# A decoder layer on one core: input squares made as the input arrives, and short chains moved in five stages

## The reference, cut to what matters

```python
h_norm = _rmsnorm(h, norm1_w)                       # decay attention
q, k = _l2norm(h_norm @ u), _l2norm(h_norm @ v)     # 16 columns each
out = gate * _causal_conv(h_norm, k_base_kernel) + einsum(A, h_norm)   # A: q k, times gamma ** distance
h2 = h + out @ proj_w.T + proj_b
x = _layernorm(x + h2 + gelu(_rmsnorm(h2, norm2_w) @ mlp_w1 + mlp_b1) @ mlp_w2 + mlp_b2)
...
Pn = _rmsnorm(P, input_norm_w)                      # cross attention: keys and values of the context,
                                                    # then 3 rounds of scores, softmax over rows, GRU
x = _layernorm(x + slots)
...
probs = softmax(x @ router_w + router_b + expert_bias)   # 8 experts, the best 2 for each row, gates normed
x = _layernorm(x + sum of gate * (gelu(x @ W1 + B1) @ W2 + B2))
```

## Time and profile before

| | us |
|---|---|
| median of 3 runs (range) | 1296.32 (1294.4 to 1298.52) |
| the profiled execution | 1293.76 |
| its span, first to last instruction | 1292.1 |
| PE, DVE, ACT, POOL busy | 1173.5, 892.4, 616.5, 258.4 |
| attention and MLP | 0 to 202 |
| context | 202.6 to 231.5 |
| three rounds of cross attention | 232 to 941.8 |
| route | 942.1 to 972 |
| experts | 972.7 to 1268 |
| combine | 1269 to 1292.1 |

### The profile page before, as it was taken

One profiled execution on the slowest core, in us unless ns is written; L12 is line 12 of the kernel. 1 busy time (PEld: TensorE's weight loads), 2 busy tenths in 40 slices (PEclk: granted clock), 3 DMA queues, 4 the chain that ended last, 5 costly groups with the idle time before them and its releaser, 6 DMA issues. The chain is left out here.

```text
span 1292.1 us, 19037 instructions
## 1 busy us (share of the span) xinstructions
PE 1173.5 (91%) x6332; PEld 982.0 (76%) x6332; DVE 892.4 (69%) x1935; ACT 616.5 (48%) x1043; POOL 258.4 (20%) x302
## 2 busy tenths in 40 slices
PE   7988998799999999999999999999736999999990
PEld 5557884688778877878787787778636999999990
DVE  4646667698745669874556987457575888888883
ACT  4345636254434344443443444433305676676672
POOL 3016001000000000000000000000024767767751
PEclk8978998899999999999999999999857999999995
DMA  7010001000010000001000000081291222322324
GB/s 285 1 51 1 33 18 65 1 1 1 1 33 1 17 9 1 1 1 27 7 17 9 1 1 1 1 337 54 71 320 31 47 41 41 49 41 41 49 33 138
DMA packets 47983, 60.54 MB, mean 47 GB/s; under 512 B 15151, under 2 KB 39153, under 8 KB 47025
## 3 DMA queue, kind: packets, MB, share of 16 engines
q1 hardware_dynamic: 37856, 45.27, 10.3%
q0 software_dynamic: 8832, 12.11, 6.0%
q10 hardware_dynamic: 1232, 2.36, 0.5%
HBM read 45.25 MB, written 14.47 MB: 46 GB/s over the span
## 5 line engine op out<-in xcount | busy, mean ns | idle before, releaser
L76 PE MATMUL x_psum<-x_sn_lo,x_kq_hi 128*128 128x512 f32 (+1 forms) x312 | 126.4, 405 | 8.2 <-PEq L1372 6.8
L76 PE MATMUL x_psum<-x_p_lo,x_v_hi 128*128 128x512 f32 (+1 forms) x312 | 125.6, 402 | 5.1 <-DVE x_p_lo L1039 5.1
L77 PE MATMUL x_psum<-x_sn_hi,x_kq_lo 128*128 128x512 f32 (+1 forms) x312 | 124.6, 399 | 0.0
L78 PE MATMUL x_psum<-x_sn_hi,x_kq_hi 128*128 128x512 f32 (+1 forms) x312 | 124.0, 397 | 0.0
L77 PE MATMUL x_psum<-x_p_hi,x_v_lo 128*128 128x512 f32 (+1 forms) x312 | 123.5, 396 | 0.0
L78 PE MATMUL x_psum<-x_p_hi,x_v_hi 128*128 128x512 f32 (+1 forms) x312 | 122.7, 393 | 0.0
L947 ACT ACTIVATE x_e<-x_e,x_inv 128x1024 f32<-128x1024 f32 (+1 forms) x39 | 44.9, 1152 | 141.7 <-DVE x_inv L1060 141.7
L76 PE MATMUL e_bank<-e_w_lo,e_g_hi 128*128 128x256 f32 x368 | 107.9, 293 | 0.1
L76 PE MATMUL e_bank<-e_xT_lo,e_w_hi 128*128 128x256 f32 x368 | 105.1, 286 | 2.1 <-DVE e_xT_lo L1879 1.4
L77 PE MATMUL e_bank<-e_xT_hi,e_w_lo 128*128 128x256 f32 x368 | 104.8, 285 | 0.0
L78 PE MATMUL e_bank<-e_xT_hi,e_w_hi 128*128 128x256 f32 x368 | 104.8, 285 | 0.0
(11 more groups left out here) (395 smaller groups left out, 3169.6 us busy)
## 6 DMA issues: line engine op xcount, KB each, us to landing
w<-in_w SPq DMA_DIRECT2D x16, 1024.0 KB, 11.0
x_E_first<-scratch_row_inv SPq DMA_DIRECT2D x3, 1024.0 KB, 4.7
sT<-in_xT ACTq DMA_DIRECT2D x4, 512.0 KB, 12.1
a_x<-in_x SPq DMA_DIRECT2D x4, 512.0 KB, 7.8
scratch_x<-a_h SPq DMA_DIRECT2D x4, 512.0 KB, 2.6
w<-scratch_total SPq DMA_DIRECT2D x4, 512.0 KB, 5.7
out<-w SPq DMA_DIRECT2D x4, 512.0 KB, 2.8
y_cxT<-in_y_cxT SPq DMA_DIRECT2D x1, 1601.0 KB, 19.5
```

The lines of the kernel that those rows point to most:

```text
L76: pe.matmul(out, w_hi, x_lo, start=start, stop=False)
L77: pe.matmul(out, w_lo, x_hi, start=False, stop=False)
L78: return pe.matmul(out, w_hi, x_hi, start=False, stop=stop)
```

## The change

1. Input squares: ACT makes those of chunks 0, 2 and 3, between its exponentials and as the chunks arrive, DVE those of chunk 1, before it waits for POOL's constants. The roots of the rows get a chain of their own, before the raw queries are read, and ACT's scaled copies wait for `qk_sb` also.
2. MLP: `second_norm(c + 1)` stands after f = 2 of chunk c (c = 1, 2) on DVE and `normed(c + 1)` after f = 3 on ACT, in place of `second_norm(c + 2)`, `normed(c + 2)` in the second product of chunk c. `last_norm` stands after f = 4.
3. Context: `wh_hi` is made after `keys_hi(2)` and `wh_lo` is POOL's first work; the bias sums come after the last `norm.spread`; DVE's eight tiles of `v_lo` are split in six and two, around `keys_lo(6)` and `(7)`.
4. Route: ACT issues the write of the gates, and makes a Gelu of one column behind it; two of the nine last steps are left in the chain, two others follow unchained, and the rest goes to the start of the experts' stage on DVE, with a wait of POOL (`row_ok`) before its first `give`.
5. Combine: one chain for 16 tiles; ACT scales the first two tiles of each chunk, DVE the last two.
6. Some tiles and semaphores of the experts' stage are allocated earlier, in `program`.

```diff
+        ON_VECTOR = range(TPC, 2 * TPC)
+        ON_SCALAR = NT - TPC
...
+            def x_squares(c):
+                act.wait_ge(ld_x[c // 2], 32)
+                for t in range(c * TPC, (c + 1) * TPC):
+                    act.activation(h2[:, t], x[:, t], ACT.Square, accum_out=ss[:, t:t + 1]).then_inc(squares, 1)
+
+            x_squares(0)
             act.wait_ge(expos, 1)
             act.activation(lg[:], lg[:], ACT.Ln).then_inc(gammas, 1)
+            x_squares(2)
             act.wait_ge(expos, 2)
             act.activation(kw[:], kw[:], ACT.Exp).then_inc(gammas, 1)
...
-            for t in range(NT // 2):
-                act.wait_ge(ld_x[t // (NT // 2)], 32)
-                act.activation(h2[:, t], x[:, t], ACT.Square, accum_out=ss[:, t:t + 1]).then_inc(squares, 1)
-
+            x_squares(3)
             act.wait_ge(rs_ok, 1)
+            act.wait_ge(qk_sb, 1)
...
+                    if f == 3 and 1 <= c < NC - 1:
+                        normed(c + 1)
...
-                    normed(c + 2)
...
+            v.wait_ge(ld_x[0], 32)
+            for t in ON_VECTOR:
+                v.scalar_tensor_tensor(out=h2[:, t], in0=x[:, t], scalar=1.0, in1=x[:, t], op0=ALU.mult, op1=ALU.mult,
+                                       accum_out=ss[:, t:t + 1]).then_inc(vsquares, 1)
             v.wait_ge(consts, 1)
...
-            v.wait_ge(squares, NT // 2)
-            v.wait_ge(vsquares, NT // 2)
+            v.wait_ge(squares, ON_SCALAR)
+            v.wait_ge(vsquares, len(ON_VECTOR))
             k.step(v.tensor_scalar(sums[:, 0:NT], ss[:], 1.0 / D, EPS_RMS, ALU.mult, ALU.add))
+            rsqrt_steps(v, k, rs[:], sums[:, 0:NT], tmp[:, 0:NT])
+            v.sem_inc(rs_ok, 1)
             k.step(v.reciprocal(inv_ms[:], sums[:, 0:NT]))
...
-                rsqrt_steps(v, k, roots[:, done], sums[:, done], tmp[:, done])
+                rsqrt_steps(v, k, roots[:, ps], sums[:, ps], tmp[:, ps])
...
-                    if f == 3 and c >= 1:
+                    if f == 2 and 1 <= c < NC - 1:
+                        second_norm(c + 1)
+                    if f == 4 and c >= 1:
                         last_norm(c - 1)
...
-                    if t == c * TPC and c + 2 < NC:
-                        second_norm(c + 2)
...
         def _(pool):
+            pool.wait_ge(wh_hi_ok, 1)
+            pool.tensor_tensor(wh_lo[:], whT[:], wh_hi[:].bitcast(F32), ALU.subtract).then_inc(wh_lo_ok, 1)
             pool.wait_ge(v_hi_ok, 2)
...
             keys_hi(2)
+            act.wait_ge(ld_g, 48)
+            act.activation(wh_hi[:], whT[:], ACT.Copy).then_inc(wh_hi_ok, 1)
             keys_hi(3)
...
             norm.spread(v, slot_rs, 3, 3)
+            v.wait_ge(ld_g, 48)
+            k.mark(v.tensor_tensor(bias[:, 0:2 * DH], bi[:, 0:2 * DH], bi[:, 3 * DH:5 * DH], ALU.add))
+            k.mark(v.tensor_copy(bias[:, 2 * DH:3 * DH], bi[:, 2 * DH:3 * DH]))
+            k.mark(v.tensor_copy(bias[:, 3 * DH:], bi[:, 5 * DH:]))
             keys_lo(3)
...
+            v.wait_ge(v_hi_ok, 1)
+            rows_lo(0, 6)
             for i in range(6, len(keys)):
                 keys_lo(i)
...
+            rows_lo(6, 8)
...
-            sp.wait_ge(gate_ok, TOP)
-            sp.dma_start(io["x2"][:, D:].rearrange("(t p) k -> p t k", p=P), gates[:]).then_inc(gate_out, 16)
             sp.wait_ge(gate_out, 16)
...
             act.activation(pr[:], lg[:], ACT.Exp).then_inc(exp_ok, 1)
+            act.wait_ge(gate_ok, TOP)
+            act.dma_start(io["x2"][:, D:].rearrange("(t p) k -> p t k", p=P), gates[:]).then_inc(gate_out, 16)
+            act.activation(warm[:], ones[:, 0:1], ACT.Gelu)
...
+            k.step(v.tensor_scalar(found_i[:], bank[7][:, 0:PLACES], -1.0, None, ALU.add))
+            k.mark(v.tensor_scalar(token_of[:], found_i[:], T - 1, None, ALU.bitwise_and))
+            v.tensor_scalar(found[:], bank[7][:, 0:PLACES], -1.0, None, ALU.add)
+            v.scalar_tensor_tensor(out=empty[:], in0=bank[7][:, 0:PLACES], scalar=0.0, in1=spare[:], op0=ALU.is_equal, op1=ALU.mult)
...
+            pool.wait_ge(row_ok, 4)
             give(0, 0)
...
+            v.tensor_scalar(second[:], found[:], float(T), None, ALU.is_ge).then_inc(row_ok, 1)
+            v.tensor_scalar(first[:], found[:], float(T), None, ALU.is_lt).then_inc(row_ok, 1)
+            v.tensor_copy(row_f[:], token_of[:]).then_inc(row_ok, 1)
+            v.wait_ge(row_ok, 3)
+            v.wait_ge(ld_e, 16 * (2 * NE + 2))
+            v.tensor_tensor(row_of[:], row_f[:], empty[:], ALU.add).then_inc(row_ok, 1)
...
-            for h, tiles in enumerate(HALVES):
-                act.wait_ge(norm_ok, h + 1)
-                for t in tiles:
+            act.wait_ge(norm_ok, 1)
+            for c in range(NC):
+                for t in range(c * TPC, c * TPC + TPC // 2):
                     act.activation(x2[:, t], x2[:, t], ACT.Identity, bias=nb[:, t:t + 1], scale=rs[:, t:t + 1]).then_inc(out_ok, 1)
...
+            norm_of_stats(v, k, list(range(NT)), mark, stats, mv, rs, tmp, nb, norm_ok)
+            v.wait_ge(norm_ok, 1)
+            for c in range(NC):
+                for t in range(c * TPC + TPC // 2, (c + 1) * TPC):
+                    v.tensor_scalar(x2[:, t], x2[:, t], rs[:, t:t + 1], nb[:, t:t + 1], ALU.mult, ALU.add).then_inc(more_ok, 1)
```

More of the change, by code:

```diff
@@ L333, in cx_squares_of @@
                 act.wait_ge(ld_cx, 32)
-                act.wait_ge(squares, NT // 2 + (c + 3) * TPC)
+                act.wait_ge(squares, ON_SCALAR + (c + 3) * TPC)
                 for m in some:
@@ L418, in queries_and_keys @@
                 ps = slice(NT + g * NT, NT + (g + 1) * NT)
-                done = slice(0 if g == 0 else ps.start, ps.stop)
                 pairs = qk[:, ts].rearrange("p t a r -> p (t a) r")
@@ L474, in second_norm @@
                 sl = slice(c * TPC, (c + 1) * TPC)
-                v.wait_ge(squares, NT // 2 + (c + 1) * TPC)
+                v.wait_ge(squares, ON_SCALAR + (c + 1) * TPC)
                 k.step(v.tensor_scalar(ss[:, sl], ss[:, sl], 1.0 / D, EPS_RMS, ALU.mult, ALU.add))
@@ L1414, in _ @@
             rows_hi(1)
-            act.wait_ge(ld_g, 48)
-            act.activation(wh_hi[:], whT[:], ACT.Copy).then_inc(wh_hi_ok, 1)
             for i in range(6, len(keys)):
@@ L1525, in route @@
     gate = [gates[:, :, i] for i in range(TOP)]
-    second, first = shared["second"], shared["first"]
+    found, empty = shared["found"], shared["empty"]
     w2, b1, b2, ld_e = (shared[n] for n in ("w2", "b1", "b2", "ld_e"))
@@ L1739, in experts @@
         room = sT[:].rearrange("p c (a n) -> p (c a) n", n=CH)
-        xg = [room[:, 2 * i:2 * i + 2].rearrange("p a n -> p (a n)")[:, 0:SH * (D + TOP)].rearrange("p (s d) -> p s d", s=SH) for i in range(2)]
+        xg = shared["xg"]
         y = [room[:, 4 + i].rearrange("p (s d) -> p s d", s=SH) for i in range(2)]
         g32 = [room[:, 6 + i].rearrange("p (f n) -> p f n", f=2) for i in range(2)]
-        second, first = shared["second"], shared["first"]
+        second, first, found, empty = shared["second"], shared["first"], shared["found"], shared["empty"]
         share = sb("share", [P, 2, 2, SH])
         shared_ok, summed = sem("shared_ok"), sem("summed")
-        tokens, rows = sb("tokens", [P, 2 * SH], I32), sb("rows", [P, 2 * SH], I32)
-        tokens_ok, rows_ok = sem("tokens_ok"), sem("rows_ok")
+        tokens, rows = shared["tokens"], sb("rows", [P, 2 * SH], I32)
+        row_f = sb("row_f", [P, PLACES])
+        tokens_ok, rows_ok, row_ok = shared["tokens_ok"], sem("rows_ok"), sem("row_ok")
         passed = sem("passed")
-        ld_x, y_out = [sem("ld_x0"), sem("ld_x1")], [sem("y_out0"), sem("y_out1")]
+        ld_x, y_out = [shared["ld_x0"], shared["ld_x1"]], [sem("y_out0"), sem("y_out1")]
         xT_mm, xT_hi_ok, xT_lo_ok, w1_hi_ok, w1_lo_ok, w2_hi_ok, w2_hi_last, w2_lo_ok = (
@@ L1874, in _ @@
         def _(v):
-            v.wait_ge(ld_e, 16 * (2 * NE + 2))
             def turn(i, slot):
@@ L1993, in combine @@
         nb, rs, tmp = sb("nb", [P, NT]), sb("rs", [P, NT]), sb("tmp", [P, NT])
-        vchain, norm_ok, out_ok, stored = (sem(n) for n in ("vchain", "norm_ok", "out_ok", "stored"))
+        vchain, norm_ok, out_ok, more_ok, stored = (sem(n) for n in ("vchain", "norm_ok", "out_ok", "more_ok", "stored"))
         loaded, BEFORE = shared["loaded"], 16
-        HALVES = [list(range(h * NT // 2, (h + 1) * NT // 2)) for h in range(2)]
         block = ctx.enter_context(nc.Block())
@@ L2022, in _ @@
             k = Chain(v, vchain)
-            for tiles in HALVES:
-                for t in tiles:
-                    if t % TPC == 0:
-                        v.wait_ge(loaded[t // TPC], BEFORE + 16)
-                    mark = k.mark(v.bn_stats(stats[:, t], x2[:, t]))
-                norm_of_stats(v, k, tiles, mark, stats, mv, rs, tmp, nb, norm_ok)
+            for t in range(NT):
+                if t % TPC == 0:
+                    v.wait_ge(loaded[t // TPC], BEFORE + 16)
```

(8 more changed lines are left out.)

32 lines of the change are left out of this document (6 added, 26 removed).

## The result

The changed kernel takes 1287.09 us, the median of 7 runs (1282.35 to 1294.98), against 1296.32 for the kernel before in the same runs; the ratio is 0.9937, with a 95% interval of 0.9915 to 0.9959. The forecast was 1283.7, the range 1275 to 1290. Ten further runs of the changed kernel had a mean of 1289.8, and the mean of all 17 is 1289.1, that of 74 further runs of the kernel before 1295.3: 6.2 us less, where 12.65 were forecast. The median of the first seven was the luckier figure. The profiled execution took 1282.35 (span 1280.6), the fastest of the 17, which has to be kept in mind when its rows are read.

A forecast was written before the change was run, and what follows sets the result against it. TensorE was taken to be busy for most of the span, so edits pay only at its standstills or where no PE work is left. Terms summed to -12.65 from 1293.76, giving 1281.1; plus 2.6 for the median, 1283.7, range 1275 to 1290.

The forecast's parts named there:

- Front: Input stage: first eviction at 21.4 instead of 24.73, -3.3 us; clock fall in the second wide pass gone, -1.7.
- Attention, -2.8: Attention, not edited but shifted: the low clock from 72.9 to 86.6 partly avoided, -2.8 us, bounds 0 and -6.4.
- rival (b): Clock takes gains back: low stretch of 72.9 returns whole, both new MLP stalls cost 2.4; 1288.7 us, chance 0.15.
- MLP, +1.9: MLP: old stalls and low clock removed, -7.9 us; two new a_n waits, +7.2, with clock falls, +2.6.
- Context, -2.6: Context stage: reordered DVE and POOL work lets wi_lo start at 226.4 to 227.0, -2.6 us, bounds 0 and -4.3.
- Rounds, 0: Three rounds of cross attention: no change forecast, 0 us.
- Route and Gelu table, -4.15: Route: gates issued from ACT, shorter DVE chain, -3.5 us; Gelu table load moved into ACT's idle time, -0.65.
- The cover that the prediction named: Experts' start: if the w2 load lands late, the gather covers about 1.5 us more.
- Last stage, 0: Last stage: earlier statistics, but stores at the loads' rate end at 1291.8 as now; 0 us, bounds -1.5 and +0.3.
- (a): MLP: the two new stalls don't appear, DVE or ACT finishing the norm before PE arrives; 1273.9 us, chance 0.12.
- (c): Context and last stage: shared ports eat the gain, a store waits longer, edits do nothing; 1289.1 us, chance 0.13.
- (d): MLP: clock stays low after both new pauses for longer than 13.7 us; 1303.9 us with 20 each, chance 0.03.

The follow-up runs named there:

- experiment 7: Kernel of experiment 2 plus 9 small matmuls filling PE's 2.56 us wait for a_n ahead of the last attention chunk; median 1274.85 us.
- experiment 9: Kernel of experiment 2 with the last five tiles of the context's v_lo moved from POOL to DVE, seven there in all; median 1274.3 us.
- 10: Kernel of experiment 2 with both the filler matmuls at the experts' start and seven tiles of v_lo on DVE; median 1271.24 us.
- 8: Kernel of experiment 2 plus 11 and 4 filler matmuls on PE around the first transposition of the experts' stage; median 1275.32 us.
- experiment 2: Changed kernel with squares and one root chain for chunks 2 and 3 before the MLP's first Gelu and g_lo, n2 scaling back at chunk end; median 1276.11 us.
- Experiments 1 to 3: First: changed kernel, MLP edits undone, 1284.89 us; second: see experiment 2; third: changed kernel, 22 and 14 filler matmuls in PE's a_n waits, 1286.35 us.
- experiment 6: Kernel before with one stage's edits alone, three kernels: context, median 1291.22 us; route and experts' start, 1296.28; last stage, 1294.8.

## Why the prediction came out, point by point

The number was within 0.3% of the median of the first seven runs, though above the 1279 to 1287 that had the chance of 0.50. That is in part luck. Against the mean of all 17 runs it is 5.4 us too low, and the gain was half of the forecast one. Input and attention gave 1.0 instead of 7.8 and the MLP cost 5.6 instead of 1.9; the rounds and the last stage, put at nothing, gave 2.1 and 1.4. Over all profiled executions, where the code of a stage was the same (with old and new code):

| stage | old code | new code | mean difference |
|---|---|---|---|
| input and attention | 83.1 to 87.0 (4) | 78.65 to 90.8 (9, without experiment 7) | -1.0 |
| MLP | 118.4 to 119.2 (6) | 124.16, 124.72 | +5.6 |
| context | 29.4 to 30.3 (4) | 26.4 to 27.7 (8, without 9 and 10) | -2.9 |
| rounds | 709.2 to 710.6 (4) | 705.3 to 711.3 (10) | -2.1 |
| route | 30.3 to 30.6 (4) | 26.5 (10) | -3.9 |
| experts | 296.3 to 296.7 (4) | 295.6 to 298.5 (8, without 8 and 10) | +0.2 |
| last stage | 23.0 to 23.1 (4) | 21.5 to 21.9 (10) | -1.4 |

Their sum, before rounding, is -5.6, and the means of the runs differ by 6.2.

- **Front.** The steps up to the eviction were right: 21.5, and 21.8 to 22.8 where x landed later. The step that failed is the pause of PE: it was worked out from the end of the first wide pass in before, 20.17, which had run at a low clock; at full clock it ends at 18.5, and the pause is 3.6 to 4.9. The clock fall behind it was away only in the first profile of the changed kernel, its fastest execution. In the other nine profiles with this front the second pass took 9.4 to 11.0 us, where kernels with the old front have 9.5 to 10.7, and not 8.0.
- **Attention, -2.8.** It came as 0. The fall returned in each profile with the new front, for 13.6 to 17.1 us, except where the wait of 2.56 was filled. From the eviction to the MLP the clock was low for 22.9 us on the mean of the nine profiles, for 19.7 in the four with the old front, and that stretch took 1.3 us longer. So the front's gain of 2.3 us at the eviction (22.2 instead of 24.5 on the mean) is worth 1.0 at the MLP. Why the low time is longer stays open. That part of rival (b) is what happened. PE's pause right ahead of the fall, which the prediction didn't name, is one that the change leaves as it is:

```profile
72.36 1.39 PE L612 MATMUL a_psum<-ident,a_n 128*128 128x128 f32 x8 [2.56 <-ACT a_n L305]
```

- **MLP, +1.9.** It measured +5.6. Mis-sized: the first wait, 5.50 for 3.6, and the clock, about 4.8 for 2.6. The step behind the first: the chain was priced at its length without POOL, at chunk 1's place in the old kernel, although the edit's own gain moves chunk 1 to where POOL still adds. What the old stall cost was near right, 8.5 (before against experiment 2) for 7.9. Experiments 1 to 3 show the waits and the clock.
- **Context, -2.6.** Right in size and way, -2.3 in the first profile. The rule on the shared ports (the Trainium skill, SBUF — State Buffer, Who interferes with whom) is borne out by the rows 3.44 beside 3.45 and by experiment 9.
- **Rounds, 0.** The step that is missing: the context stage's chain is shorter, so PE's pause at its end is 3.6 instead of 6.8 (2.6 in experiments 9 and 10), and the low clock after it 0 to 6.8 us instead of 6.8 to 10.2. In 13 of the 14 profiles the rounds' time less half of the low time in them is 695.9 to 697.0 (694.5 in the other), so nearly all of their variation is clock. Of the 2.1 us on the mean, 1.8 is half of the low time right behind that pause, 1.6 us inside the rounds instead of 5.2. The 4.75 of the first profile had two later falls less as well, at places where the code is the same. The four executions with the long pause have 709.2 to 710.6, the ten with the short one 705.3 to 711.3, so it is a tendency of few executions, not a settled amount.
- **Route and Gelu table, -4.15.** The stage gave 3.9 to 4.0 and the wait of 0.65 is gone, but the experts' stage is 0.2 longer, not 0.65 shorter. The cover that the prediction named, the gather, holds while the weights end DVE's wait within about 2.6 us; the step that was left out is that what stands behind them on DVE then collides with POOL's copies, which costs PE 2 us (experiment 6). That explains 2 of the 3.4 us that the kernel with the route alone did not gain; the rest is 1.2 us, as much as ten runs can tell.
- **Last stage, 0.** It gave 1.4, at the far bound. The rate of the stores was right (the first issue 1273.30, 2.8 to land, then 3 x 1.45 gives 1280.45; it was 1280.2). Mis-sized: the loads, in 7.8 us after the first issue and not 9, so that the statistics end at 9.3 and not 10.5. Before had 9.0 too, but it is one of two long ones: the 14 profiles have 7.8 to 9.7, twelve of them under 8.2.
- **Rivals.** (a) fell, (c) and (d) too; (b) is true of its two mechanisms. Its 1288.7 is nearer to the mean of all 17 runs, 1289.1, than the forecast is; what the front lost beyond it, the rounds and the last stage made good.

## What to carry to other kernels

A chain that stands in the way of one wait should go to a stretch where its engine is idle for longer than the chain, not to the next place in the same loop: two squares' groups and one chain of eight columns, moved to where ACT waited 10.6 and DVE 4.4 us, gave 13.5 us against the changed kernel and took 8.5 off the MLP of the kernel before, while the move by one chunk cost 3 to 6. When a pause of PE is worked out, both its ends must be taken at the same clock. And a profile's one execution can be 7 us off the mean here: compare single stages over several kernels that share their code.
